# Second attention's second pass: the weighing waits by halves of heads, and ScalarE casts the values of every tile

## What is computed

```python
def _L1_xattn_ref(x, context, Wq, Wk, Wv, Wo, bo):
    q = x @ Wq
    k = context @ Wk
    v = context @ Wv
    q = q.reshape(B, Nq, HEADS, DIM_HEAD).transpose(0, 2, 1, 3)
    k = k.reshape(B, Nk, HEADS, DIM_HEAD).transpose(0, 2, 1, 3)
    v = v.reshape(B, Nk, HEADS, DIM_HEAD).transpose(0, 2, 1, 3)
    sim = jnp.einsum('bhid,bhjd->bhij', q, k) * SCALE
    attn = jax.nn.softmax(sim, axis=-1)
    out = jnp.einsum('bhij,bhjd->bhid', attn, v)
    out = out.transpose(0, 2, 1, 3).reshape(B, Nq, INNER_DIM)
    return out @ Wo + bo
...
x = x + _L0_xattn_ref(_layernorm(x, axis=-1), ctx_768, ...)
x = x + _L0_attn_ref(_layernorm(x, axis=-1), ...)
x = x + _L0_ffn_ref(_layernorm(x, axis=-1), ...)
x = x + _L1_xattn_ref(_layernorm(x, axis=-1), ctx_768, ...)
x = x + _L1_attn_ref(_layernorm(x, axis=-1), L1_attn_W)
x = x + _L1_ffn_ref(_layernorm(x, axis=-1), ...)
```

## Time and profile before

| | us |
|---|---|
| median of 3 runs | 1446.17 |
| lowest and highest | 1443.87, 1449.4 |
| the profiled execution, own time | 1446.07 |
| its span | 1444.3 |
| TensorE busy | 1360.1 (94%) |
| VectorE busy | 1111.1 (77%) |
| ScalarE busy | 1070.2 (74%) |
| chain that ended last: TensorE's share | 84% |

### The profile page before, as it was taken

One profiled execution on the slowest core, in us unless ns is written; L12 is line 12 of the kernel. 1 busy time (PEld: TensorE's weight loads), 2 busy tenths in 40 slices (PEclk: granted clock), 3 DMA queues, 4 the chain that ended last, 5 costly groups with the idle time before them and its releaser, 6 DMA issues.

```text
span 1444.3 us, 37910 instructions
## 1 busy us (share of the span) xinstructions
PE 1360.1 (94%) x15595; PEld 899.9 (62%) x15595; DVE 1111.1 (77%) x1678; ACT 1070.2 (74%) x1590; POOL 198.9 (14%) x196
## 2 busy tenths in 40 slices
PE   5888889999999999999999979999999999999989
PEld 2445456666777694333333357777777777777768
DVE  5677678998000777999999988888888888888864
ACT  3667665666997466888888868888888787888841
POOL 6333210000000006000000000000000004341630
PEclk9999999999999999999999999999999999999999
DMA  4457549564664574556655566788777689898910
GB/s 144 174 198 239 180 151 233 137 141 116 168 170 136 205 246 147 191 187 226 216 189 192 188 134 132 152 154 154 146 144 143 117 176 184 177 188 172 226 70 5
DMA packets 137138, 240.01 MB, mean 166 GB/s; under 512 B 10412, under 2 KB 120710, under 8 KB 136966
## 3 DMA queue, kind: packets, MB, share of 16 engines
q1 hardware_dynamic: 136966, 237.58, 62.4%
HBM read 159.30 MB, written 78.23 MB: 164 GB/s over the span
## 4 chain that ended last, share of the span: by engine, by line
PE 84%; DVE 8%; ACT 3%; issue 3%; POOL 1%; DMA 0%; SPq 0%; POOLq 0%; DVEq 0%; ACTq 0%
PE ps L847 83%; DVE W L1617 2%; ACT W L1391 2%; DVE W L1587 1%; DVE p L1587 1%; DVE q_all L1587 1%; DMA W<-in_ctx_dram 0%; PE ps L886 0%; ACT ps L1367 0%; DVE q_all L1915 0%; POOL q_all L767 0%; ACT p L1367 0%; DVE att L1587 0%; DVE v L1587 0%; DVE v L1762 0%
## 5 line engine op out<-in xcount | busy, mean ns | idle before, releaser
L1367 ACT ACTIVATE p<-ps 128x512 f16<-128x512 f32 (+1 forms) x490 | 329.3, 682 | 94.9 <-PE ps L847 93.7
L1587 DVE TENSOR_TENSOR p<-ps,p 128x512 f16<-128x512 f32 (+1 forms) x467 | 350.7, 752 | 61.9 <-ACT ps L1367 59.4
L847 PEld LDWEIGHTS ps<-q_all,W 128*128 128x128 f16 (+1 forms) x3544 | 230.4, 99 | 70.4 <-issue 5.6
L847 PE MATMUL ps<-q_all,W 128*128 128x128 f16 (+2 forms) x3544 | 265.3, 226 | 7.5 <-DVE p L1587 4.4
L1367 ACT ACTIVATE ps<-ps 128x512 f32<-128x512 f32 x392 | 235.8, 602 | 0.0
L847 PE MATMUL ps<-v,p 128*128 128x130 f16 x3136 | 169.8, 206 | 7.2 <-DVE p L1587 2.7
L847 PE MATMUL ps<-wv,ctxT_a_hi 128*128 128x512 f16 (+1 forms) x588 | 156.0, 347 | 12.8 <-DVE W L1617 10.0
L847 PEld LDWEIGHTS ps<-v,p 128*128 128x128 f16 x3136 | 147.5, 97 | 14.3 <-issue 4.8
L1587 DVE TENSOR_TENSOR v<-ps,v 128x512 f16<-128x512 f32 x196 | 135.4, 691 | 17.7 <-ACT v L1464 5.3
L847 PE MATMUL ps<-wv,ctxT_b 128*128 128x512 f16 (+1 forms) x504 | 137.0, 340 | 0.0
L1700 DVE TENSOR_REDUCE W<-ps 128x1 f32<-128x448 f32 x224 | 125.0, 616 | 11.5 <-PE ps L847 11.5
(11 more groups left out here) (279 smaller groups left out, 2037.9 us busy)
## 6 DMA issues: line engine op xcount, KB each, us to landing
W<-keys_hi SPq DMA_DIRECT2D x54, 896.0 KB, 8.2
W<-keys_low SPq DMA_DIRECT2D x27, 896.0 KB, 11.5
keys_hi<-p SPq DMA_DIRECT2D x75, 224.0 KB, 1.9
keys_low<-p SPq DMA_DIRECT2D x75, 224.0 KB, 1.9
keys_hi<-W SPq DMA_DIRECT2D x65, 224.0 KB, 2.1
keys_low<-W SPq DMA_DIRECT2D x65, 224.0 KB, 1.9
W<-values SPq DMA_DIRECT2D x28, 484.0 KB, 4.2
W<-in_L_ffn_W_dram SPq DMA_DIRECT2D x10, 1024.0 KB, 10.7
```

The costliest lines, as they stand in the source:

```text
L847: return pe.matmul(out_, lhsT, rhs, start=start, stop=stop, **kw)
L1367: return act.activation(out_, in_, ACT.Exp, scale=scale)
L1587: return dve.tensor_tensor(out_, a, b, op)
```

## The change

Three edits, all in that pass:

- `weigh1` no longer waits for `exped`, and waits for `low_made` twice: ahead of head 0 for half 0 of its tile, ahead of head 4 for half 1.
- ScalarE casts the values of every tile, not of odd tiles only, ahead of the exponentials of that tile.
- VectorE's cast on even tiles goes; its subtraction waits for ScalarE's cast on every tile. The semaphore `values_hi_act` goes, and ScalarE counts `values_hi`.

```diff
             def weigh1(g, t):
                 i, b = g * NT + t, t % 2
-                pe.wait_ge(exped, n_scored1(g, t, 1))
                 pe.wait_ge(values_made, i + 1)
-                pe.wait_ge(low_made, 2 * i + 2)
...
                 for h in range(8):
+                    if h % 4 == 0:
+                        pe.wait_ge(low_made, 2 * i + h // 4 + 1)
...
-                        if i % 2:
-                            act.wait_ge(values_summed, i + 1)
-                            if i >= 2:
-                                act.wait_ge(weighed, NT + i - 1)
-                            act.copy(v_tile(i)[:, :, 0:L1.dh],
-                                     v_bank(i).rearrange("p (h c) -> p h c", h=8)).then_inc(values_hi_act, 1)
+                        act.wait_ge(values_summed, i + 1)
+                        if i >= 2:
+                            act.wait_ge(weighed, NT + i - 1)
+                        act.copy(v_tile(i)[:, :, 0:L1.dh],
+                                 v_bank(i).rearrange("p (h c) -> p h c", h=8)).then_inc(values_hi, 1)
...
             def split_values1(i):
                 v4 = v_tile(i)
                 vp = v_bank(i).rearrange("p (h c) -> p h c", h=8)
-                if i % 2 == 0:
-                    dve.wait_ge(values_summed, i + 1)
-                    if i >= 2:
-                        dve.wait_ge(weighed, NT + i - 1)
-                    dve.tensor_copy(v4[:, :, 0:L1.dh], vp).then_inc(values_hi, 1)
-                    dve.wait_ge(values_hi, i // 2 + 1)
-                else:
-                    dve.wait_ge(values_hi_act, i // 2 + 1)
+                dve.wait_ge(values_hi, i + 1)
                 tt(v4[:, :, L1.dh + 2:L1.vw], vp, v4[:, :, 0:L1.dh], ALU.subtract).then_inc(values_made, 1)
```

More of the change, by code:

```diff
@@ L148, in perceiver_kernel @@
         keys_summed, keys_hi, keys_low = (sem(n) for n in ("keys_summed", "keys_hi", "keys_low"))
-        values_summed, values_hi, values_hi_act, values_made = (
-            sem(n) for n in ("values_summed", "values_hi", "values_hi_act", "values_made"))
+        values_summed, values_hi, values_made = (sem(n) for n in ("values_summed", "values_hi", "values_made"))
         values0_summed, values0_out = sem("values0_summed"), sem("values0_out")
```

## The result

The changed kernel took 1432.82 us (median of 4 runs, 1432.39 to 1433.7) against 1445.75 us of the kernel before beside it. The ratio is 0.9895, with a 95% interval of 0.9881 to 0.991. On another chip it was 0.9886 (0.9871 to 0.99). The gain is 13 us where 9.5 were forecast, and the time lies 0.2 us under the range's lower end of 1433.0. The span of the profiled execution is 1431.3 us.

The account below looks back on a forecast made before the run. TensorE was taken as the bound, with small stalls its busy time hides. Gains of 7.0 + 0.6 + 0.7 + 0.8 + 0.35 = 9.5 us from 1446.2 gave 1436.7 us, range 1433 to 1441.5.

Parts of the forecast that it names:

- The wait by halves: Steady stretches: second half's rest has 0.27 us margin, so the 0.08 us stall in 89 even tiles goes; 7.0 us.
- even tiles on TensorE pay 0.08 us for what odd tiles do on ScalarE: Steady stretches: ScalarE's cast ahead of an odd tile's exponentials makes its last rest, hence its weighing, 0.08 us late.
- The waits named issue: Steady stretches: 3.5 us in the second and under 1 us in the first, taken as unchanged.
- The cast on ScalarE: Every tile: ScalarE's five instructions take 2.47 us by starts, so tiles repeat at TensorE's 2.67 us, ScalarE at 93%.
- Rival A: Whole pass: ScalarE becomes the bound above 0.542 us between starts; 55 us slower, 1501, if instructions did not overlap; chance 0.06.
- First tiles, 0.6: First nine tiles: VectorE's dropped cast nets 0.2 us, the half weighing starting early 0.35; 0.6 us gained.
- Between the groups and tile 103, 0.7 + 0.8: VectorE's dropped casts shorten the scores' 2.62 us wait between groups by 0.7 and tile 103's 3.48 us by 0.8.
- The clock: First tiles and between groups: falls to half speed cost at most 1.7 us each; change taken as 0, +-1.7 for range.
- rival C: Disturbed places give more: no clock fall between the groups, first tiles up to 1.5 more; 12 to 13 us, 1433.7; chance 0.11.
- The end, 0.35: Last weighing, which waited 1.42 us: its first half runs while the last rest is made; 0.35 us gained.

Follow-up runs that it names:

- casts_only: Kernel before with ScalarE's cast in every tile alone; the weighing still waits for both halves ahead of head 0: 1452.6 us, ratio 1.0031.
- late_between: Changed kernel with VectorE's cast of the values put back in one tile, the first of group 1: 1433.5 us, one run; tiles 99 to 104 took 20.24 us.
- halves_only: Kernel before with the wait by halves alone, VectorE still casting values of even tiles: 1435.4 us, ratio 0.9906.
- halves_again: Same kernel as halves_only, run a second time, beside the changed kernel on one chip: 1437.1 us, ratio 0.9928.

## Why the prediction was right or wrong

The terms of the forecast that had a number came out at 9.5 us, as forecast. It failed by two terms that were put at nothing, the issue waits and the clock.

- **The wait by halves**: right in size, 6.9 us (11.0 less 4.1 of issue waits). 240.30 us for the 90 tiles was forecast as 240.3.
- **Its cause**: wrong. The step "even tiles on TensorE pay 0.08 us for what odd tiles do on ScalarE" fell with casts_only: with the cast in every tile the loss was the same and not double. The rest of half 1 is late in every tile; a late tile shields the next. The size was right because it was counted from rows (89 tiles of 0.08 us), whatever the cause.
- **"The waits named issue are in that ... and do not change"**: this is the step that failed with the largest sum. They fell from 4.1 and 5.8 us to 1.0 to 2.3, 2.9 us in the first comparison, because TensorE's queue no longer stands still ahead of each weighing and its instructions are loaded earlier.
- **The cast on ScalarE**: right. 2.77 us with half a cast more give 2.50 for the five. Rival A did not happen: starts stay 0.48 to 0.52 us apart, under its threshold of 0.542.
- **First tiles, 0.6**: right by the two traces with a fall in either kernel, 33.77 - 33.09 = 0.7.
- **Between the groups and tile 103, 0.7 + 0.8**: right, 2.62 to 1.89 us of waiting and 3.48 to 2.67. Without a fall of the clock on either side it is 19.48 - 18.08 = 1.4 us.
- **The clock, "I take 0"**: wrong for the fall between the groups. It was gone in all three traces of the changed kernel, 1.4 us by late_between (2.2 less 0.7) and 1.6 by the two traces of halves_only and halves_again. That was rival C in part, to which the forecast gave 0.11. The first tiles' and the last part's falls are chance: a gain of 1.7 us and a loss of 2.0 in the first comparison, so they nearly cancelled there.
- **The end, 0.35**: 0.42.

For the two first traces the sum closes: 9.5 + 2.9 + 1.4, with 1.7 for the missing fall in the first tiles, less 0.5 at the begin and 2.0 behind the pass, is 13.0 us. The chance terms nearly cancel, so that the time ended just outside the range is an accident of their size; that the gain is larger than forecast is no accident, for the second comparison gave 16.6 us, of which 9.5 + 3 + 1.4 = 13.9 are explained and some 2.7 are not accounted for.

## What to carry to other kernels

A wait placed ahead of a block of matmuls can cost twice: the stall that the starts show, and the lead that the queue loses, 6.9 and some 3 us here. Move it to the first instruction that needs it, also where the stall looks tiny. When a stall alternates, ask whether a late tile shields the next before giving it a cause in what differs between them. A shortened wait may be worth more than its length where the granted clock has been falling with it, 2.2 us for 0.7 here.

## What was not expected of the hardware

- TensorE's waits named issue go with how far its queue runs ahead: 4.1, 5.8 and 9.9 us in 181 tiles with 0.06 us of lead, 4.6 with 0.24, 1.0 to 2.3 with 0.94, in the kernel before at places that repeat to 0.01 us.
- These waits end 1.3 to 1.8 us behind the end of a 16 KB packet of the queue named instruction, 45 times of 46.
- ScalarE's instruction reads 0.60 us at 93% load and 0.88 at full load, with 0.48 between starts in both.
- A VectorE instruction on 8 columns of SBUF took 2.40 us beside a memset of GpSimd and 0.17 without.
